# A fused attention kernel on one core: half of the mirrored Gram block left out, normalisations moved in ScalarE's queue, the mask copied into the score banks

## The reference

```python
q = Wq @ y + bq; k = Wk @ y + bk; v = Wv @ x + bv            # y = ctx, 8 heads of 32 channels
scores = einsum('bhdl,bhel->bhde', q, k) / sqrt(256)         # channel by channel, summed over positions
o = Wo @ (softmax(scores) @ v) + bo + x                      # layer 0
x = (o - mean) * rsqrt(var + 1e-5) * gn_w + gn_b             # mean and var over the whole sample
# layer 1: attention in chunks of 64 positions, q = k = v = ctx, 8 heads
scores = einsum('bnqhd,bnkhd->bnhqk', qh, kh) / sqrt(32) + where(mask_of_key > 0, 0.0, -1e9)
out = (softmax(scores) @ vh) @ W_out.T + b_out
out = out.transpose(0, 2, 1) * mask + x
x = (out - mean) * rsqrt(var + 1e-5)                         # over the positions of each channel
```

## Time and profile before

| | us |
|---|---|
| median of 3 runs | 1607.18 (1606.38 to 1608.31) |
| the profiled execution, its own time | 1603.11 |
| its span, first to last instruction | 1601.0 |
| mean granted clock of TensorE, share of full | 0.994 |
| ACT busy in the span | 985.2 |
| DVE busy | 1324.3 |
| POOL busy | 460.0 |

### The profile page before, as it was taken

The page is one execution under the profiler, slowest core; times in us unless marked ns, Lnnn a source line. Parts: engine busy times, 40 slices in busy tenths (PEclk is TensorE's granted clock), DMA queues, the critical chain, the costliest instruction groups (busy, mean ns, idle before and its releaser), DMA issues.

```text
span 1601.0 us, 53789 instructions
## 1 busy us (share of the span) xinstructions
PE 1553.0 (97%) x23816; PEld 1307.3 (82%) x23816; DVE 1324.3 (83%) x2008; ACT 985.2 (62%) x1780; POOL 460.0 (29%) x292
## 2 busy tenths in 40 slices
PE   7999999999999999999999999999999999999994
PEld 6888888888888888888888888888888888888873
DVE  4778879888798888979888788888978879888886
ACT  5556665656657666575565666566576665756743
POOL 1114233141331414224142331413314132141422
PEclk9999999999999999999999999999999999999998
DMA  6122331423323242241423314233142422414121
GB/s 239 58 98 75 107 110 48 143 81 114 106 76 119 68 140 81 92 128 42 147 84 97 115 53 146 76 119 107 55 137 70 131 90 81 125 57 140 41 67 66
DMA packets 96326, 157.20 MB, mean 98 GB/s; under 512 B 5344, under 2 KB 38240, under 8 KB 95968
## 3 DMA queue, kind: packets, MB, share of 16 engines
q1 hardware_dynamic: 96096, 153.78, 30.5%
HBM read 120.20 MB, written 33.55 MB: 96 GB/s over the span
## 4 chain that ended last, share of the span: by engine, by line
PE 88%; ACT 6%; DVE 4%; issue 1%; DMA 0%; POOL 0%; DVEq 0%; SPq 0%; POOLq 0%; ACTq 0%
PE pj_ps L281 42%; PE l_ps L281 11%; PE s_ps L305 7%; PE w_ps L316 6%; PE l_ps L389 6%; PE w_ps L334 6%; DVE yt_hl L698 3%; PE s_ps L294 2%; ACT o_sb L581 2%; PE l_ps L405 2%; PE l_ps L425 2%; ACT prob_t L568 1%; ACT yt_hl L540 1%; ACT prob L573 1%; PE l_ps L413 1%
## 5 line engine op out<-in xcount | busy, mean ns | idle before, releaser
L933 POOL TENSOR_TENSOR prob<-prob,row_inv 128x1024 f32<-128x1024 f32 x128 | 262.3, 2049 | 958.9 <-DVE row_inv L729 958.9
L591 ACT CAST att_hi<-w_ps 128x256 fp32r<-128x256 f32 x256 | 82.9, 378 | 252.7 <-PE w_ps L334 247.0
L281 PE MATMUL pj_ps<-y_hi,w_hi 128*128 128x512 f32 x512 | 208.5, 407 | 9.3 <-DVE y_lo L694 9.3
L281 PE MATMUL pj_ps<-y_hi,w_lo 128*128 128x512 f32 x512 | 202.2, 395 | 0.0
L281 PE MATMUL pj_ps<-y_lo,w_hi 128*128 128x512 f32 x512 | 202.2, 395 | 0.0
L724 DVE TENSOR_REDUCE row_sum<-prob 128x16 f32<-128x1024 f32 x128 | 154.9, 1210 | 47.5 <-ACT prob L573 47.5
L698 DVE TENSOR_TENSOR yt_hl<-yt_raw,yt_hl 128x1024 fp32r<-128x1024 f32 x64 | 117.4, 1834 | 83.4 <-ACT yt_hl L540 83.4
L712 DVE TENSOR_REDUCE row_max<-s_ps 128x16 f32<-128x1024 f32 x128 | 155.7, 1216 | 22.2 <-PE s_ps L305 21.1
L950 POOL TENSOR_TENSOR o_sb<-o_sb,u_sb 128x1024 f32<-128x1024 f32 x63 | 164.4, 2631 | 2.8 <-ACT o_sb L581 2.8
L568 ACT COPY prob_t<-w_ps 128x512 f32<-128x512 f32 x256 | 149.6, 585 | 21.6 <-PE w_ps L316 17.5
L719 DVE TENSOR_TENSOR prob<-s_ps,row_max 128x1024 f32<-128x1024 f32 x128 | 155.4, 1214 | 0.1
(11 more groups left out here) (107 smaller groups left out, 3519.8 us busy)
## 6 DMA issues: line engine op xcount, KB each, us to landing
y_raw<-in_ctx SPq DMA_DIRECT2D x64, 512.0 KB, 4.9
yt_raw<-in_ctx_t SPq DMA_DIRECT2D x64, 512.0 KB, 4.8
x_raw<-in_x SPq DMA_DIRECT2D x64, 512.0 KB, 5.0
out_z<-o_sb SPq DMA_DIRECT2D x64, 512.0 KB, 3.6
mask_b<-in_mask SPq DMA_DIRECT2D x64, 256.0 KB, 4.0
u_sb<-in_w SPq DMA_DIRECT2D x2, 512.0 KB, 5.0
w_sb<-in_w SPq DMA_DIRECT2D x1, 1024.0 KB, 10.9
cst<-in_consts SPq DMA_DIRECT2D x1, 512.0 KB, 7.0
```

Source lines behind the costliest of these rows:

```text
L281: last = mm(dst, lhs, rhs, start=i == 0, stop=i == len(todo) - 1)
L933: nc.gpsimd.tensor_tensor(cut, cut, row_inv[:, u % 2, :].unsqueeze(2).to_broadcast([P, 2 * HEADS, CHUNK]), ALU.mult).then_inc(probs_done, 1)
```

## The change

The mask products and neg_rows are gone. Instead the flags are f32 and already multiplied by -1e9 / SCALE1, and ACT copies them, spread over the heads, into the two score banks (`preset_mask`, two copies of 128 by 512 per unit) behind the exponents of the unit before; `scores` then adds its 64 products to what stands there and waits for mask_set. Two products at the very start, of raw weights that are overwritten, open the banks. The Gram products of half i = 1 leave out their first 128 columns, which are the mirror of a block that half 0 has; the transposes of hl are three instead of four, and the missing block of the finished matrix is transposed from its mirror in slot 6 (`S_SUM`) and copied to gram by ACT in slot 7 (`copy_lower`), which now gives gram_done. `group_normed` runs for q = 0 and 1 at the end of slots 2 and 3, and for q = 2 and 3 at the start of slots 4 and 6.

```diff
@@ -33,6 +33,7 @@
...
 EPS = 1e-5
+UPPER = ((0, 0), (0, 1), (1, 1))
 W_HALF = 2 * HALVES * E
...
@@ -46,7 +47,7 @@
...
-T_X1, T_Z, T_Z_STATS, T_STAT, T_FINAL, T_STORE = 1, 3, 4, 8, 10, 10
+T_Z, T_Z_STATS, T_STAT, T_FINAL, T_STORE = 3, 4, 8, 10, 10
...
@@ -68,7 +69,6 @@
...
         mean_mat = cst[:, C_MEAN:C_MEAN + P]
-        neg_rows = sb("neg_rows", [P, CHUNK], BF16)
         w0_sb = sb("w0_sb", [P, 4, HALVES, E])
...
@@ -93,7 +93,7 @@
...
         v_s = sb("v_s", [P, 2, PAIRS, E])
-        blocked = sb("blocked", [P, 2, BT], BF16)
+        blocked = sb("blocked", [P, 2, BT])
...
@@ -144,7 +144,7 @@
...
         wqk_in, wvo_in, cols_in, consts_in, w0_in = sem("wqk_in"), sem("wvo_in"), sem("cols_in"), sem("consts_in"), sem("w0_in")
-        neg_done = sem("neg_done")
+        banks_open, mask_set = sem("banks_open"), sem("mask_set")
         consts_done = sem("consts_done")
...
@@ -163,6 +163,7 @@
...
         wout_ready, u_done = sem("wout_ready"), sem("u_done")
+        upper_done, lower_ready = sem("upper_done"), sem("lower_ready")
         gram_ready, hl_copied, gram_half = sem("gram_ready"), sem("hl_copied"), sem("gram_half")
...
@@ -285,16 +286,7 @@
...
                     pe.wait_ge(qkv_copied, count(n, 24, 6 * b + 3))
-                    pe.wait_ge(blocked_done, count(n, 4, b))
-                if exists(n, 8, u - 1):
-                    pe.wait_ge(shifted, count(n, 8, u - 1))
-                for i in range(4):
-                    r, h = divmod(i, 2)
-                    rows = slice(DH * i, DH * i + DH)
-                    mm(s_ps[64 * h:64 * h + 64, r].rearrange("p j g c k -> p j g (c k)"), neg_rows[rows, :],
-                       blocked[rows, b % 2, e * UT:(e + 1) * UT].rearrange("p (j t) -> p j t", j=2).unsqueeze(2).to_broadcast([DH, 2, HALVES, P]),
-                       start=True, stop=False)
-
+                pe.wait_ge(mask_set, count(n, 8, u))
...
@@ -303,7 +295,7 @@
...
                             last = mm(s_ps[64 * h:64 * h + 64, r, t // 2, g, t % 2, :], q_s[rows, b % 2, g, cut], k_s[rows, b % 2, g, cut],
-                                      start=False, stop=t == 3 and g == HALVES - 1)
+                                      start=False, stop=True, skip_group_check=True)
                 last.then_inc(scores_ready, 1)
...
@@ -385,18 +377,21 @@
...
                 for lb in range(PAIRS):
+                    hi_lo = yt_hl[:, lb, :, :].rearrange("p a c -> p (a c)")
                     for i in range(HALVES):
-                        last = mm(l0_ps[i][:, :].rearrange("p (a c) -> p a c", a=2), yt_hl[:, lb, 0, i * P:(i + 1) * P], yt_hl[:, lb, :, :],
+                        last = mm(l0_ps[i][:, i * P:], yt_hl[:, lb, 0, i * P:(i + 1) * P], hi_lo[:, i * P:],
                                   start=q == 0 and lb == 0, stop=q == BLOCKS - 1 and lb == PAIRS - 1)
...
                     pe.wait_ge(gram_half, count(n, 1, 0))
-                    for i in range(HALVES):
-                        for k in range(HALVES):
-                            last = nc.tensor.transpose(l0_ps[0][:, i * E + k * P:i * E + (k + 1) * P], hl[:, k, i * P:(i + 1) * P], ident)
+                    for i, k in UPPER:
+                        last = nc.tensor.transpose(l0_ps[0][:, i * E + k * P:i * E + (k + 1) * P], hl[:, k, i * P:(i + 1) * P], ident)
                     last.then_inc(hlt_ready, 1)
+                elif s == S_SUM:
+                    pe.wait_ge(upper_done, count(n, 1, 0))
+                    nc.tensor.transpose(l0_ps[0][:, E:E + P], gram[:, 0, P:E], ident).then_inc(lower_ready, 1)
                 elif s == S_T1:
...
@@ -449,6 +444,11 @@
...
+            pe.wait_ge(wqk_in, 16)
+            w_raw = u_sb[:, :, :].rearrange("p h t -> p (h t)")
+            for r in range(2):
+                last = mm(s_ps[:, r].rearrange("p j g c k -> p (j g c k)"), w_raw[:, 0:P], w_raw[:, 0:512], start=True, stop=True)
+            last.then_inc(banks_open, 1)
             pe.wait_ge(w_hi_done, 1)
...
@@ -466,7 +466,6 @@
...
             last.then_inc(c1_ready, 1)
-            pe.wait_ge(neg_done, 1)
             pe.wait_ge(w0_in, 2 * 16)
...
@@ -572,6 +571,19 @@
...
+            def preset_mask(n, u):
+                b, e = divmod(u, 2)
+                if e == 0:
+                    act.wait_ge(blocked_done, count(n, 4, b))
+                if exists(n, 8, u - 1):
+                    act.wait_ge(shifted, count(n, 8, u - 1))
+                else:
+                    act.wait_ge(banks_open, 1)
+                for r in range(2):
+                    last = copy(s_ps[:, r].rearrange("p j g c k -> p j g (c k)"),
+                                blocked[:, b % 2, e * UT:(e + 1) * UT].rearrange("p (j t) -> p j t", j=2).unsqueeze(2).to_broadcast([P, 2, HALVES, P]))
+                last.then_inc(mask_set, 1)
+
             def group_normed(n, q):
...
@@ -611,6 +623,10 @@
...
                 last.then_inc(hl_copied, 1)
+
+            def copy_lower(n):
+                act.wait_ge(lower_ready, count(n, 1, 0))
+                copy(gram[:, 1, 0:P], l0_ps[0][:, E:E + P]).then_inc(gram_done, 1)
...
@@ -629,6 +645,7 @@
...
                 copy_k(0, 0, g)
+            preset_mask(0, 0)
             for m in range(2):
...
@@ -641,16 +658,18 @@
...
                         copy_att(n, u - LAG)
+                    if not first and s in (4, 6):
+                        group_normed(n - 1, s // 2)
                     if e == 1 and not (first and u == 0):
...
                         copy_hl(n)
+                    if s == S_SUM + 1:
+                        copy_lower(n)
                     if s == S_SC + 1:
...
                         copy_output(n, s - S_MX)
-                    if e == 1 and not first and T_X1 <= s < T_X1 + BLOCKS:
-                        group_normed(n - 1, s - T_X1)
                     if S_X <= s < S_X + BLOCKS:
...
@@ -665,12 +684,14 @@
...
                         exponents(n, u)
+                        if not (last and u + 1 >= UNITS):
+                            preset_mask(n, u + 1)
                     if j == 1 and not (last and b + 2 >= BLOCKS):
...
                         copy_u0(n)
-                    if e == 0 and not first and T_X1 <= s < T_X1 + BLOCKS:
-                        group_normed(n - 1, s - T_X1)
+                    if not first and s in (2, 3):
+                        group_normed(n - 1, s - 2)
                     if s == SLOTS - 1 and not last:
...
@@ -704,8 +725,8 @@
...
                 if exists(n, 8, 2 * (b - 2) + 1):
-                    dve.wait_ge(scores_ready, count(n, 8, 2 * (b - 2) + 1))
-                nc.vector.tensor_scalar(blocked[:, b % 2, :], mask_b[:, b % 4, :], 0.0, None, ALU.is_le).then_inc(blocked_done, 1)
+                    dve.wait_ge(mask_set, count(n, 8, 2 * (b - 2) + 1))
+                nc.vector.tensor_scalar(blocked[:, b % 2, :], mask_b[:, b % 4, :], 0.0, NEG / SCALE1, ALU.is_le, ALU.mult).then_inc(blocked_done, 1)
...
@@ -745,11 +766,13 @@
...
                     for i in range(HALVES):
-                        last = tt(gram[:, i, :], l0_ps[i][:, 0:E], hl[:, i, :], ALU.add)
+                        last = tt(gram[:, i, i * P:], l0_ps[i][:, i * P:E], hl[:, i, i * P:], ALU.add)
                     last.then_inc(gram_half, 1)
...
                     dve.wait_ge(hlt_ready, count(n, 1, 0))
-                    tt(gram[:, :, :], l0_ps[0][:, :].rearrange("p (i c) -> p i c", i=HALVES), gram[:, :, :], ALU.add).then_inc(gram_done, 1)
+                    for i in range(HALVES):
+                        last = tt(gram[:, i, i * P:], l0_ps[0][:, i * E + i * P:(i + 1) * E], gram[:, i, i * P:], ALU.add)
+                    last.then_inc(upper_done, 1)
                 elif s == S_T1:
...
@@ -852,10 +875,6 @@
...
             flags(0, 0)
-            dve.wait_ge(consts_in, 16)
-            for i in range(4):
-                last = nc.vector.tensor_copy(neg_rows[DH * i:DH * i + DH, :], cst[0:DH, C_NEG:C_NEG + CHUNK])
-            last.then_inc(neg_done, 1)
             split_y(0, 1)
...
```

## The result

The changed kernel takes 1584.9 us (median of 4 runs, 1583.19 to 1585.95) against 1606.78 us for the kernel before, run beside it (1603.4 to 1608.31): a ratio of 0.9867 with a 95% interval of 0.9855 to 0.988. That is 21.9 us less, where 30.7 less was forecast. The profiled execution took 1583.99 us, its span is 1582.2.

What follows compares the result with a forecast made beforehand. PE's own stream was taken as the bound. 1.68 + 0.89 + 0.10 - 0.40 - 0.35 = 1.92 us per sample, times 16 = 30.7, gave 1576.5 us; inner range 1568 to 1584 (chance 0.55), full range 1562 to 1593.

Steps and rivals of the forecast that it cites:

- T1: Slot 7: T1 now needs copy_lower, which comes late in ACT's queue; PE waits 0.40 us per sample.
- Mask price: Mask products delay PE by 0.24 us per unit, less 0.03 for weight loads: 0.21, or 1.68 us per sample.
- Gram pitch: Gram products of 384 columns start 0.175 us apart, between 0.23 and 0.12; 16 products gain 0.89 us per sample.
- rival B: The Gram pitch hardly falls: 1586 us with the skill's slope, 1591 with none; chance 0.06.
- Copies into PSUM: Two ACT mask copies per unit take 0.47 us of queue each, 7.6 us per sample; ends 0.40 and 0.70 a copy.
- rivals C: ACT's copies cost 0.70 us like its activations: 1598 us, or 1607 with the lower mask price; chance 0.10.
- The failed step: List of what becomes late: two new PE waits per sample, 0.40 us in slot 7 and 0.35 in slots 9 to 10.
- Second place: Slots 9 to 10: transposes wait for att_lo behind a nearly full ACT queue, 0.35 us more per sample.
- The normalisations: Eight activations per sample issued later, at no cost; PE's 0.7 us wait for the last Gram part shrinks by 0.10.
- all other units have more: Mask copies finish about 0.7 to 1 us early at unit 2 to 3, earlier elsewhere, so mask_set costs nothing.
- Rival A: ACT and DVE waits are covered after all; full gain with 0.24 per unit, 1562 us; chance 0.22.
- Rival D: Dearer ACT copies delay three places: slower by over 0.2% at 0.82 us a copy, 1627 at 1.0; chance 0.07.

Runs made afterwards that it cites:

- f2: Changed kernel with DVE doing the layer-0 softmax normalisation of slot 9 before the reciprocal that releases POOL; 1578.8 us, ratio 0.9825.
- the version with three new orders: Changed kernel with slot-11 layer-0 weights before the scaling, layer-0 normalisation before POOL's release, and copy_lower before the mask copies; 1563.39 us, ratio 0.9728.
- g2: Changed kernel without its Gram part, keeping the mask copies and the moved normalisations; 1594.78 us, ratio 0.9933.

## Why the prediction was right, and where it was not

The time, 1584.9, lies in the stated range and the direction was the forecast one; the gain was 8.8 us smaller than forecast (by the medians; 8.4 counted from 1576.5 itself), and the time is 0.9 above the inner range that had the chance 0.55. That it came this near is partly luck: the waits behind ACT and DVE were 0.9 us per sample worse than worked out, and a wait that was given 0.10 brought 0.8. By its terms, in us per sample:

| term | predicted | measured |
|---|---|---|
| mask products off PE | 1.68 | 1.44 (8 x 0.18) |
| Gram products | 0.89 | 0.88 (4 x 0.22) |
| last Gram part waits less | 0.10 | 0.8 |
| T1 waits for the lower block | -0.40 | -0.4 |
| transposes of slot 10 wait | -0.35 | -0.64 |
| weights of slot 12 wait | none | -0.60 |
| sum | 1.92 | 1.5 by terms, 1.33 by the period |

- **Mask price.** The difference of the two weight loads, 32 ns, was too small a correction: the score products themselves now take 1.09 us from their first start to that of the next group, as the rows at the end of this section show, where they took 1.03 (708.74 to 709.77). Why they take 0.06 longer no run shows. The measured 0.18 lies inside the bounds. The terms add up to 0.15 more than the period shows, spread over the units and a few irregular samples.
- **Gram pitch.** The middle between two measured pitches was right: products of 384 columns start 0.175 us apart in the trace, those of 512 columns 0.231 to 0.237. The slope in the Trainium skill, TensorE: Matmul & The Clock Gate, section Back-to-back issue gap, would have given 0.27; the trace disagrees, and rival B falls.
- **Copies into PSUM.** They take 601 ns, the copies from PSUM beside them 595:

```profile
L583 ACT COPY s_ps<-blocked 128x512 f32<-128x512 f32 x256 | 142.8, 601 | 0.0
L567 ACT COPY prob_t<-w_ps 128x512 f32<-128x512 f32 x256 | 152.1, 595 | 12.6 <-PE w_ps L308 12.5
```

In the queue a copy takes 0.52 (728.50 to 729.53 for two), where 0.47 was taken. So the price was well taken from the nearest row, and rivals C and D fell in the form they had. The sentence of the Trainium skill, ScalarE: Activation LUTs, section Step-by-step: what each stage is for, that PSUM is the faster destination for ScalarE doesn't show in these rows; they differ in the source too, so they don't refute it. The scores never waited for mask_set.
- **T1** came out as worked: name, place and size, shown by putting copy_lower first. (The 1.75 us by which PE and ACT come earlier is 1.83 by its own terms; both sides of the comparison use it, so the 0.40 doesn't change.)
- **The failed step** is the list of what becomes late. It followed ACT alone and took DVE's durations as fixed: 0.35 was worked out for slot 10 and 0.64 measured, nothing for slot 12 and 0.60 measured. In "Second place" the a_max idle was counted, but not that the layer-0 exponents, once behind mask copies, let DVE's multiplication lose a race against POOL that it had won by 0.02 us; with that race mended (f2) 0.23 is left, nearer to the 0.35. Slot 12 was not walked through at all, where x_lo loses such a race and DVE is late. Together 0.9 us per sample, 14 us of the total.
- **The normalisations** were costed as a move that gives 0.10. Alone they give 12.8 us; the prediction kept POOL's join as the cause of the 3.23 us and did not see that an earlier cast would bring the subtraction ahead of the join. This made up for 11 us of the 14. And "all other units have more" was true for mask_set but not for what stands behind the mask copies: only the moved normalisations kept copy_pt from being late.
- Rival A is refuted as it stood (the waits were not covered), but the version with three new orders reaches 1563.4, near the time it gave. (Its 0.93 is 0.99 by its own terms, 0.40 + 0.35 + 8 x 0.03, and its time 1561.) Rival B's 1586 is nearer to the measured time than the forecast is, with a mechanism that the trace refutes. Rival D gave "slower" to expensive copies. The mask part alone is slower than before at the ordinary price, through the queue behind the copies.

The timeline, PE, first score product of a unit and first product of the group behind, in the changed kernel and, third, the latter before:

```profile
699.74 1.16 PE L297 MATMUL s_ps<-k_s,q_s 32*64 32x64 f32 x64
700.83 0.86 PE L326 MATMUL w_ps<-prob_t,v_s 64*32 64x64 f32 x64
...
709.77 0.86 PE L334 MATMUL w_ps<-prob_t,v_s 64*32 64x64 f32 x64
```

What stays open: the 0.23 us of slot 10 was not tried by itself, and neither was the order of ACT's x_hi and the mask copies in slot 10, which by the rows sets who starts first, x_lo or POOL.

## What to carry to other kernels

Work taken off a bounding engine and put on one that is 62% busy is paid where that engine's queue is locally full, and by the instructions queued behind it, not by its own result being late; here the mask part saved some 1.4 us per sample on PE and cost more until three orders were mended. When a change shifts DVE against POOL by a tenth of a microsecond, walk through every place where both touch SBUF, because here the loser of the race waited for a whole instruction. Read such a place in more than one sample: the order can differ between them. Judge parts of a change together as well as alone: the same move was worth 12.8 us in one kernel and 38 in another.

## What the runs showed of the hardware

- DVE and POOL in SBUF: the multiplication of a took 0.42 us when it started 0.02 before POOL's row scaling and 2.08 when it started 0.10 after it; the subtraction x_lo 1.16 at 0.16 before and 2.97 at 0.01 after; the subtraction of yt 1.28 at 0.16 before the join and 3.23 at 0.22 after. The scaling of o_sb took 0.99 for a pair alone and 2.58 beside POOL.
- The granted clock in the tail: behind waits of 0.6 to 1.6 us between short pieces of work, the last products of most traces ran at about half the rate (0.43 us apart, the 1.2 GHz level), and in those of the kernel before, the normalisations alone, and Gram and normalisations 0.23 us apart behind the same waits. The mean clock also differs from run to run of one kernel (0.991 to 0.994 before). What decides was not found.
- The same at the start: the two bank-opening products give PE work while it used to wait. In nine of the ten traces of kernels that have them, most of the first projections run 0.23 us apart; in the tenth, the one without the Gram part (g2), they run 0.43 apart in spite of them (9.90, 10.33). In the four traces of kernels without them, the kernel before among them, the first six or more gaps are 0.43. The changed kernel:

```profile
9.65 0.39 PE L282 MATMUL pj_ps<-y_lo,w_hi 128*128 128x512 f32 x1
9.88 0.40 PE L282 MATMUL pj_ps<-y_hi,w_lo 128*128 128x512 f32 x1
```
